# A decoder layer for 32 sequences: another mapping of rows to partitions, and another order of the setup

## What is computed

```
x = x + attn(layernorm(x))               # 16 heads of 32; out @ Wff.T + bff
x = x + xattn(ctx, ctx, layernorm(x))    # one head; scores over 750 context rows
x = x + ffn(layernorm(x))                # see below
def ffn(h):
    scores = (h @ q_proj.T @ router.T) @ (keys @ router.T).T / sqrt(48) + mask   # 2048 keys
    top, idx = top_k(scores, 8)
    agg = softmax(top) @ values[idx]                                         # 8 rows of 512
    gate = sigmoid(w * clip(0.5 * nvar + 2.5 * sigmoid(learned), 0, 5) + bias)
    return h + gate * agg    # nvar: log1p(var(h)) over its mean of all rows of all sequences
```

## Time and profile before

| | us |
|---|---|
| median of 3 executions | 2807.72 (2807.22 to 2808.9) |
| the profiled execution | 2788.23 |
| its span | 2786.2 |
| TensorE busy | 2556.4 (92%) |
| VectorE busy | 2146.0 (77%) |
| ScalarE busy | 1431.3 (51%) |
| GpSimd busy | 683.1 (25%) |
| moved | 358.87 MB in 131542 packets |

### The profile page before, as it was taken

How to read it: one execution, slowest core, us unless ns; L and a number is a source line. 1 busy time by engine, 2 the same in 40 slices (tenths; PEclk the granted TensorE clock), 3 DMA queues, 4 the chain that set the end, 5 groups by cost and what they waited for, 6 DMA issues and landing times.

```text
span 2786.2 us, 56938 instructions
## 1 busy us (share of the span) xinstructions
PE 2556.4 (92%) x19090; PEld 2104.0 (76%) x19090; DVE 2146.0 (77%) x4207; ACT 1431.3 (51%) x4247; POOL 683.1 (25%) x650
## 2 busy tenths in 40 slices
PE   6899999999999999999999999999999999999730
PEld 4578878887888788878887888778888887788520
DVE  5456888888888888888888888888888888887552
ACT  2345554555555545555555455555554555555252
POOL 0001222222222222222222222222222222222254
PEclk9899999999999999999999999999999999999955
DMA  5223354454544444444444445444445454444799
GB/s 189 53 80 80 107 132 121 128 137 130 133 121 112 130 125 123 138 131 131 128 111 128 131 113 138 131 131 131 115 126 134 106 139 130 132 130 111 202 205 178
DMA packets 131542, 358.87 MB, mean 129 GB/s; under 512 B 21906, under 2 KB 26514, under 8 KB 123267
## 3 DMA queue, kind: packets, MB, share of 16 engines
q0 software_dynamic: 63520, 160.60, 24.4%
q1 hardware_dynamic: 63188, 192.15, 23.6%
q10 hardware_dynamic: 4784, 5.46, 0.6%
HBM read 316.37 MB, written 41.78 MB: 129 GB/s over the span
## 4 chain that ended last, share of the span: by engine, by line
PE 74%; DVE 8%; ACT 7%; issue 7%; DMA 2%; POOL 1%; DVEq 0%; ACTq 0%; POOLq 0%; SPq 0%
PE psX L1144 43%; PE psA L1144 13%; PE psA L1153 5%; PE psF L1144 4%; PE psA L1210 4%; DVE top L999 3%; PE psA L1233 2%; ACT paT L640 2%; PE psX L1153 2%; ACT sc L640 1%; DMA vg<-in_L_ffn_aux_values,idx 1%; ACT xT_hi L663 1%; DVE xmax L948 1%; PE psF L1153 1%; DVE idx L1002 1%
## 5 line engine op out<-in xcount | busy, mean ns | idle before, releaser
L589 POOL DMA_INDIRECT vg<-in_L_ffn_aux_values,idx x512 | 491.7, 960 | 1550.5 <-DVE agg L1028 1053.8
L684 ACT ACTIVATE pa<-psA,nmax 112x224 f32<-112x224 f32 x1024 | 444.6, 450 | 197.8 <-DVE nmax L917 194.5
L917 DVE TENSOR_REDUCE nmax<-psA 112x4 f32<-112x896 f32 x256 | 267.1, 1085 | 100.9 <-PE psA L1210 100.9
L1144 PE MATMUL psX<-big,gT 128*112 128x375 f32 x1024 | 333.4, 478 | 0.6 <-ACT gT L711 0.6
L1028 DVE SCALAR_TENSOR_TENSOR agg<-vg,wt,agg 112x512 f32<-112x512 f32 x406 | 303.8, 748 | 9.2
L1144 PE MATMUL psX<-pT,cx 125*128 125x224 f32 x1536 | 299.1, 355 | 0.0
L1144 PEld LDWEIGHTS psX<-pT,cx 125*128 125x128 f32 x1536 | 288.0, 190 | 4.0 <-issue 0.3
L932 DVE TENSOR_TENSOR pa<-pa,rsum 112x896 f32<-112x896 f32 x256 | 279.4, 1091 | 8.8
L1144 PEld LDWEIGHTS psX<-big,gT 128*112 128x112 f32 x1024 | 175.2, 176 | 126.0 <-issue 0.9
L1153 PE MATMUL psA<-ident,pa 112*112 112x112 f32 x2048 | 227.2, 262 | 19.5 <-DVE oT_lo L895 19.4
L640 ACT COPY paT<-psA 112x448 f32<-112x448 f32 x512 | 237.2, 560 | 11.4 <-PE psA L1153 9.4
(11 more groups left out here) (220 smaller groups left out, 5957.0 us busy)
## 6 DMA issues: line engine op xcount, KB each, us to landing
big<-in_ctx_t SPq DMA_DIRECT2D x32, 1500.0 KB, 8.1
cx<-in_ctx SPq DMA_DIRECT2D x32, 1344.0 KB
xa<-in_x SPq DMA_DIRECT2D x64, 224.0 KB
centered<-in_x_t SPq DMA_DIRECT2D x32, 448.0 KB, 4.6
x<-in_L_attn_bff POOLq DMA_DIRECT2D x32, 448.0 KB, 5.7
x<-cb_scratch POOLq DMA_DIRECT2D x32, 448.0 KB, 5.9
x<-in_x SPq DMA_DIRECT2D x31, 448.0 KB
out<-x SPq DMA_DIRECT2D x30, 448.0 KB, 3.1
```

The source lines that it names most:

```text
L589: pool.indirect_dma_start(vg[:, c % SLOTS, k, :], None, aux_values, bass.IndirectOffsetOnAxis(ap=idx[:, t, n:n + 1], axis=0))\
L684: last = nc.scalar.activation(pa[:, t, h, :], psA[0:R, h, t * S:(t + 1) * S], ACT.Exp, bias=nmax[:, k % 2, h, t:t + 1], accum_out=rsum[:, ...
L917: nc.vector.tensor_reduce(nmax[:, k % 2, h:h + 2, :], psA[0:R, h:h + 2, 0:T * S].rearrange("p h (t s) -> p h t s", t=T), AX_X, ALU.max, ne ...
L1144: last = nc.tensor.matmul(dst, stationary, moving, start=n == 0, stop=n == len(pairs) - 1)
```

## The change

1. All sequences are laid out with `pairs`: rows 2r and 2r + 1 in partition r, for the residual x, the output, agg and the transposed x of the host. Loads and stores of a whole sequence then move 4 KB of adjoining bytes for each partition, where they moved two pieces of 2 KB. The stores of agg still move one 2 KB row for each partition. The biases come from DRAM scratch with the row twice (`bff_scratch`, new, and `cb_scratch`), so that they too are read as 4 KB. The moments are stored transposed, number by number.
2. x for the moments is one transfer instead of two.
3. The query weights' load goes from SyncE's queue to the head of ScalarE's; the value weights' load waits until the query weights have landed.
4. FIRST: the query and key weights are split ahead of the first centering. SETUP: the split of wff and the third m2 product go from after the 7th A step to after the 9th.

```diff
-FIRST = (("N", "norm", 0), ("N", "spread", 0), ("W", "mean", 0), ("N", "center", 0), ("W", "split", 0),
-         ("W", "mean", 1), ("W", "mean", 2), ("W", "split", 1), ("W", "split", 2), ("W", "keys", 0),
+FIRST = (("N", "norm", 0), ("N", "spread", 0), ("W", "mean", 0), ("W", "split", 0), ("W", "mean", 1),
+         ("W", "split", 1), ("N", "center", 0), ("W", "mean", 2), ("W", "split", 2), ("W", "keys", 0),
...
-         7: (("W", "m2", 1), ("W", "wff", 0), ("W", "m2", 2),),
+         7: (("W", "m2", 1),),
+         9: (("W", "wff", 0), ("W", "m2", 2),),
...
-        moments_dram = nc.dram_tensor("moments_scratch", [B, R, T], F32).ap()
-        cb_dram = nc.dram_tensor("cb_scratch", [1, D], F32).ap()
+        moments_dram = nc.dram_tensor("moments_scratch", [B, T, R], F32).ap()
+        cb_dram = nc.dram_tensor("cb_scratch", [T, D], F32).ap()
+        bff_dram = nc.dram_tensor("bff_scratch", [T, D], F32).ap()
...
-            return v.partition_broadcast(R).unsqueeze(1).to_broadcast([R, T, D])
-
-        def tiles(a):
-            return a.rearrange("(t r) d -> r t d", r=R)
+            return v.rearrange("t d -> (t d)").partition_broadcast(R).rearrange("r (t d) -> r t d", t=T)
...
-                for t in range(T):
-                    sp.dma_start(xa[:, t, :], pairs(row(x, b))[:, t, :]).then_inc(x_loaded, 16)
+                sp.dma_start(xa[:, :, :], pairs(row(x, b))).then_inc(x_loaded, 16)
...
-            sp.dma_start(staged[0], rows(attn_wq_t)).then_inc(weight_loaded[0], 16)
...
-                sp.dma_start(row(moments_dram, b), rstd["N"][:, :]).then_inc(moments_stored, 16)
+                with nc.allow_non_contiguous_dma(reason="moments, one by one"):
+                    sp.dma_start(row(moments_dram, b).rearrange("t r -> r t"), rstd["N"][:, :]).then_inc(moments_stored, 16)
...
-                sp.dma_start(tiles(row(out, b)), x2[:, :, :]).then_inc(base_stored, 16)
+                sp.dma_start(pairs(row(out, b)), x2[:, :, :]).then_inc(base_stored, 16)
...
-                sp.dma_start(late[k], tiles(row(agg_dram, n))).then_inc(late_loaded[k], 16)
+                sp.dma_start(late[k], pairs(row(agg_dram, n))).then_inc(late_loaded[k], 16)
...
-                pool.dma_start(x1[:, :, :], over_rows(attn_bff), accum_op=ALU.add).then_inc(xr_biased, 16)
+                pool.dma_start(x1[:, :, :], over_rows(bff_dram), accum_op=ALU.add).then_inc(xr_biased, 16)
...
-                pool.dma_start(tiles(row(out, n)), late_tile[n], accum_op=ALU.add).then_inc(late_stored[k], 16)
+                pool.dma_start(pairs(row(out, n)), late_tile[n], accum_op=ALU.add).then_inc(late_stored[k], 16)
...
+            act.dma_start(staged[0], rows(attn_wq_t)).then_inc(weight_loaded[0], 16)
             act.dma_start(staged[1], rows(attn_wk_t)).then_inc(weight_loaded[1], 16)
+            act.wait_ge(weight_loaded[0], 16)
             act.dma_start(staged[2], rows(attn_wv_t)).then_inc(weight_loaded[2], 16)
...
-            act.dma_start(x1[:, :, :], tiles(row(x, 0))).then_inc(xr_loaded, 16)
+            act.dma_start(bff_dram, attn_bff.partition_broadcast(T)).then_inc(bff_stored, 16)
+            act.dma_start(x1[:, :, :], pairs(row(x, 0))).then_inc(xr_loaded, 16)
...
-    a = np.asarray(inputs["x"]).reshape(B, S, C, P).transpose(0, 3, 2, 1)
+    a = np.asarray(inputs["x"]).reshape(B, R, T, C, P).transpose(0, 4, 3, 2, 1)
```

More of the change, by code:

```diff
@@ L257, in build @@
         x_loaded, xt_loaded, xr_loaded, ctx_loaded, cxT_loaded = (sem(f"{n}_loaded") for n in ("x", "xt", "xr", "ctx", "cxT"))
-        moments_stored, moments_spread, cb_stored = sem("moments_stored"), sem("moments_spread"), sem("cb_stored")
+        moments_stored, moments_spread = sem("moments_stored"), sem("moments_spread")
+        cb_stored, bff_stored = sem("cb_stored"), sem("bff_stored")
         xt_scaled, xT_split, xr_biased = sem("xt_scaled"), sem("xT_split"), sem("xr_biased")
@@ L447, in first_cxT @@
                 sp.dma_start(big[:, :], row(ctx_t, 0)).then_inc(cxT_loaded, 16)
-                sp.dma_start(cb_dram, cb[0:1, :]).then_inc(cb_stored, 16)
+                sp.dma_start(cb_dram, cb[0:T, :]).then_inc(cb_stored, 16)
             def first_ctx(*_):
@@ L476, in spread_moments @@
                 wait(sp, xt_scaled, b)
-                sp.dma_start(spread[:, :], row(moments_dram, b).rearrange("r t -> (r t)").partition_broadcast(P))\
+                sp.dma_start(spread[:, :], row(moments_dram, b).rearrange("t r -> (t r)").partition_broadcast(P))\
                     .then_inc(moments_spread, 16)
@@ L494, in next_xr @@
                 wait_drained(sp, "X", FILL["X", "out", T - 1], b - 1)
-                sp.dma_start(x1[:, :, :], tiles(row(x, b))).then_inc(xr_loaded, 16)
+                sp.dma_start(x1[:, :, :], pairs(row(x, b))).then_inc(xr_loaded, 16)
             def store_whole(_, n):
@@ L499, in store_whole @@
                     sp.wait_ge(merged, n - WHOLE + 1)
-                    sp.dma_start(tiles(row(out, n)), late_tile[n]).then_inc(late_stored[LATE + n - DIRECT], 16)
+                    sp.dma_start(pairs(row(out, n)), late_tile[n]).then_inc(late_stored[LATE + n - DIRECT], 16)
             def store_base(b, _):
@@ L511, in store_agg @@
                     sp.wait_ge(summed, CHUNKS * b + c + 1)
-                    sp.dma_start(tiles(row(agg_dram, b))[:, t, :], agg[:, :]).then_inc(agg_stored, 16)
+                    sp.dma_start(pairs(row(agg_dram, b))[:, t, :], agg[:, :]).then_inc(agg_stored, 16)
             def load_agg(_, n):
@@ L562, in bias_x @@
             def bias_x(b, _):
+                if isinstance(b, int) and b == 0:
+                    pool.wait_ge(bff_stored, 16)
                 pool.wait_ge(xr_loaded, 16 * (b + 1))
                 apart(pool)
-                pool.dma_start(x1[:, :, :], over_rows(attn_bff), accum_op=ALU.add).then_inc(xr_biased, 16)
+                pool.dma_start(x1[:, :, :], over_rows(bff_dram), accum_op=ALU.add).then_inc(xr_biased, 16)
             def bias_x1(b, _):
@@ L571, in bias_x1 @@
                 apart(pool)
-                pool.dma_start(x1[:, :, :], over_rows(cb_dram.rearrange("a d -> (a d)")), accum_op=ALU.add).then_inc(x1_biased, 16)
+                pool.dma_start(x1[:, :, :], over_rows(cb_dram), accum_op=ALU.add).then_inc(x1_biased, 16)
             def add_base(b, _):
@@ L861, in x_moments @@
             def x_moments(b, _):
-                dve.wait_ge(x_loaded, 16 * T * (b + 1))
+                dve.wait_ge(x_loaded, 16 * (b + 1))
                 statistics("N", b, xa, rstd["N"][:, :])
```

## The result

| | before | after |
|---|---|---|
| median of the runs, us | 2807.47 (2806.89 to 2808.9) | 3013.82 (3011.28 to 3020.03) |
| span of the profiled execution | 2786.2 | 3013.9 |
| mean granted clock of TensorE | 0.971 | 0.932 |

What follows compares the result with a forecast made beforehand. The prediction took the loop to be bound by TensorE, busy 92% of the span. Gains of 1.8 + 5.9 + 0 + 2 = 9.7 us gave 2798.0 us from 2807.7, with an 8-in-10 range of 2788 to 2805.

Steps and rivals of the forecast that it cites:

- Part 3: Main loop: TensorE hides the larger transfers, and the single-number moments store stays within 1.2 us to spare; 0 us.
- Rival 3: Main loop: the store of single numbers lands late, 0.8 us in each of 30 passes; 14 us slower, 2822 us; chance 0.08.
- part 2: Second centering near 90 us: TensorE's 3.5 us wait goes and its clock stays up, 2.4 more; 5.9 us gained.
- Part 1: Start: weight splits ahead of the centering bring TensorE's first product from 39.7 to 37.9 us; 1.8 us gained.
- Rival 1: Start: ScalarE is free early, at 17.6, so TensorE starts at 29.5; 18.1 us gained, 2789.6 us; chance 0.13.
- the sixteen products: Sixteen TensorE records at the second centering: 7.2 us instead of 9.58 if TensorE does not stop, 2.4 us gained.
- Part 4: End, last 47 us: thirteen adding stores to out go faster with 4 KB packets; 2 us gained.
- the quarter: End: share taken of the 7.9 us upper bound on faster adding stores, giving 2 us.
- Rival 2: Second centering and end: TensorE's clock falls anyway and larger packets give nothing; 5.3 us gained, 2802.4 us; chance 0.15.
- rival 4: First pass: the earlier start is taken back and the gap at 90 us only moves; about 2 us left, 2805.7; chance 0.06.

Runs made afterwards that it cites:

- With pairs: The changed kernel with the moments stored as 112 pairs again and the centering's multiply reading them with a stride: 2775.88 us against 2783.31, ratio 0.9976.
- Single numbers alone: The kernel before, with only the moments' store, scratch order, spread order and multiply's view changed to 224 single numbers: 3035.12 us, ratio 1.0906.
- setup alone: The kernel before, with only the wff split and third m2 product moved from the 7th to the 9th step: 4.3 us less, ratio 0.9986.
- the rest on SyncE: The changed kernel with moments in pairs and ScalarE's last eleven transfers issued by SyncE behind the first spread: 2765.34 us, ratio 0.9941.

## Why the prediction was wrong

**Part 3 is the step that failed**, in the sentence "I expect a few tenths, so nothing". I had found the right place and the right margin: 8.39 us, 7.2 needed, 1.2 to spare. I bounded the new store by how long the engines move packets (1.50 us for 240 of 2 KB, so tiny ones "can hardly need more"). That bound is true of the packets, 0.13 us, and says nothing of the landing, which is what the next instruction waits for. The rows already showed it: 2.9 us to land 0.9 KB was not time of moving. A measured landing whose cause is not in the rows cannot be scaled by the rows on packets. Doubled for twice the pieces it would have been 5.8, past the margin, and the range should have reached over that; even so it would have been too low. The store measures 7.4 us alone in the kernel before and 7.1 to the next issue in the changed kernel, and the spread went from 4.3 to 5.5. What costs is that its pieces begin 4 bytes apart: as many, 512 bytes apart, land in 1.9.

**Rival 3 came true**, given 0.08 and 2822 us. Its place and its threshold were right. Its size was off in two terms. The overshoot was 4.2 us, not 0.8, as the landing was not 4.9. And "each further tenth costs 0.1 us" was wrong by a factor of 1.6 to 1.8: TensorE's clock falls behind the wait. With both, 4.2 x 1.8 x 31 = 234, for 226 from the first store to the last. I had used that very mechanism in part 2 (clock of 0.70 behind a wait of 3.50 us), and did not carry it over to the loop. The rule of the Trainium skill that I set beside this rival (one descriptor for each element) pointed at the right line, but not at the cause: as many separate pieces are fast when they lie apart.

**Part 1**: right as a sum for these edits alone (37.9 forecast, 37.50 measured), and 1.5 us of total for 1.8. In the changed kernel it failed with the store: ScalarE's first arithmetic at 32.09 for a forecast of about 25. With pairs it is 27.26, so 4.8 us of the delay went with the store's form. Two more comparisons go the same way. Single numbers alone has the start of the kernel before and of setup alone, but its first arithmetic comes at 27.87 for their 24.30 and 25.29, as one issue takes 7.16 us for 4.04 and 4.51. The kernel with a packed store behind the spread has 33.15 for 27.26. Not all of such a difference need be the packing, as the kernel with one more store of pairs has 29.73. The other 2.5 us I missed by seeing no reason why the queue should be free later: 0.7 of them is the issue of the bias copy, 1.17 us for the 0.5 that I had put; the runs do not settle how much of the rest is chance. **Rival 1** did not happen in the change, but its working was right: with ScalarE free at 17.6 the first product was to come at 29.5; in the kernel with the rest on SyncE it came at 30.14.

**Part 2**: right in mechanism and place, for this edit alone: the wait went, the clock stayed at 1.00, and the sixteen products took 7.13 us for the 7.2 forecast. The total moved by 4.3 us for 5.9, with an interval that takes both in. In the changed kernel the late start left 0.78 us of the wait and 8.30 us for the products. **Part 4**: the layout gave 1.8 us for 2, and the profiles show about 4 us less behind the last product. That the two totals agree is luck: the quarter was a choice, the interval of the 1.8 reaches from 0.3 to 5.3 us, and it takes in the whole layout, not only the end. By the Trainium skill's 512 bytes for line rate ("DMA: Bandwidth & Descriptors", Specifications) it would have been nothing; the trace does not agree, as at the end of the kernel an adding packet of 4 KB takes 328 ns in the median and two of 2 KB take 356. **Rival 2 and rival 4** did not occur.

## What to carry to other kernels

Price a small store that something waits for by its landing, never by its packets or bytes, and when its form changes, treat the landing as unknown. Let the pieces of such a store begin at least 16 bytes apart, or join them into pieces of 16 bytes (1.6 us here); if an order has to be turned, turn it where the data is read by an engine (the strided multiply cost nothing). And a wait of TensorE in a loop that was nearly without gaps cost close to double its length, so that each microsecond of lateness cost some 50 us in 31 rounds, and 10 us at the start brought 8.

## What the runs showed that I had not expected

- Landing of a store of 0.9 KB: 8.2 us as 224 packed numbers, 3.0 as 112 packed pairs, 1.9 as 224 numbers 512 bytes apart.
- Such a store, waited for by nobody, made a transfer of 1500 KB issued some 4 us behind it land in 14.4 us, not 8.1, and cost 69 us in all.
- An issue of a 2 KB transfer can hold its queue for 4 to 10 us while large transfers are under way (10.44 us for `bvc` in the changed kernel); what matters is which engine's arithmetic stands behind it.
